# Diagonal masks of attention: from VectorE's minimum on the exponentials to TensorE's addition on the scores

## The reference

```
att = einsum('bhtd,bhsd->bhts', q, k) * scale
causal = triu(ones((T, T), bool), k=1)
att = where(causal, -inf, att)
att_prob = softmax(att, axis=-1)
att_v = einsum('bhts,bhsd->bhtd', att_prob, v)
return att_v @ w_out.T + b_out
```

## Time and profile before

| | |
|---|---|
| median of 3 runs | 4427.25 us (4421.09 to 4436.3) |
| the profiled execution's own time | 4430.29 us |
| its span | 4428.6 us |
| mean granted TensorE clock | 0.907 of 2.4 GHz |
| PE busy | 3624.9 us (82%), 23244 matmuls |
| DVE busy | 2584.7 us (58%) |
| ACT busy | 1880.7 us (42%) |
| POOL busy | 834.9 us (19%) |

### The profile page before, as it was taken

One profiled execution on the slowest core, in us unless ns is written; L12 is line 12 of the kernel. 1 busy time (PEld: TensorE's weight loads), 2 busy tenths in 40 slices (PEclk: granted clock), 3 DMA queues, 4 the chain that ended last, 5 costly groups with the idle time before them and its releaser, 6 DMA issues. The chain is left out here.

```text
span 4428.6 us, 62889 instructions
## 1 busy us (share of the span) xinstructions
PE 3624.9 (82%) x23244; PEld 2176.7 (49%) x23244; DVE 2584.7 (58%) x5480; ACT 1880.7 (42%) x2902; POOL 834.9 (19%) x1018
## 2 busy tenths in 40 slices
PE   5876786778768889888893889887988988898897
PEld 3424333334256373553732666656653653663672
DVE  5746666647555464554556555455665664765764
ACT  2262361452656556464662434343126125216216
POOL 3012111120122030120300323232311220220220
PEclk8887897888889999899996989998999999999999
DMA  5312403214140000000002000002000000000000
GB/s 189 120 38 68 130 29 111 86 59 121 41 154 1 5 25 6 24 1 29 1 6 79 5 24 29 5 24 79 1 1 30 1 1 29 1 1 30 1 1 11
DMA packets 147088, 177.11 MB, mean 40 GB/s; under 512 B 16384, under 2 KB 123392, under 8 KB 146688
## 3 DMA queue, kind: packets, MB, share of 16 engines
q1 hardware_dynamic: 139008, 153.81, 11.0%
q0 software_dynamic: 6144, 16.79, 1.2%
q10 hardware_dynamic: 1632, 2.49, 0.2%
HBM read 126.40 MB, written 51.38 MB: 40 GB/s over the span
## 5 line engine op out<-in xcount | busy, mean ns | idle before, releaser
L741 DVE TENSOR_REDUCE arena<-ps 128x2 f32<-128x1024 f32 (+3 forms) x768 | 698.8, 952 | 167.7 <-PE ps L709 94.8
L937 ACT ACTIVATE arena<-ps 128x1024 f32<-128x1024 f32 (+3 forms) x768 | 577.4, 812 | 236.9 <-PE ps L846 187.1
L1020 DVE TENSOR_TENSOR arena<-arena,tri 128x256 f32<-128x256 f32 x512 | 209.0, 422 | 329.1 <-ACT arena L937 317.4
L846 PE MATMUL ps<-arena 64*128 64x512 f16 (+3 forms) x1536 | 260.0, 353 | 139.4 <-ACT arena L937 89.4
L937 ACT ACTIVATE attention<-ps 128x1024 f32<-128x1024 f32 (+3 forms) x384 | 287.9, 809 | 187.3 <-PE ps L846 187.3
L863 PE MATMUL ps<-arena 128*17 128x512 f32 (+3 forms) x3072 | 349.4, 529 | 14.3 <-DVE arena L1020 12.2
L2591 ACT ACTIVATE arena<-ps 128x256 f32<-128x256 f32 x192 | 63.6, 381 | 620.2 <-PE ps L2533 575.0
L846 PEld LDWEIGHTS ps<-arena 64*128 64x128 f16 x1536 | 71.3, 94 | 496.2 <-ACT arena L937 387.5
L863 PE MATMUL ps<-attention,live 128*33 128x512 f32 (+3 forms) x1536 | 290.6, 502 | 0.0
L709 PE MATMUL ps<-arena 64*128 64x512 f16 (+3 forms) x1536 | 237.3, 335 | 50.4 <-DVE arena L741 31.6
L1190 PE MATMUL ps<-gated_parts,weight_parts 128*128 128x256 f32 x1536 | 219.0, 300 | 30.0 <-DVE operands L1291 30.0
(11 more groups left out here) (330 smaller groups left out, 7054.0 us busy)
## 6 DMA issues: line engine op xcount, KB each, us to landing
arena<-w_experts SPq DMA_DIRECT2D x128, 256.0 KB
acc<-sums SPq DMA_DIRECT2D x16, 1024.0 KB, 5.7
x_next<-sums SPq DMA_DIRECT2D x16, 1024.0 KB, 8.3
arena<-slots_x SPq DMA_DIRECT2D x32, 512.0 KB, 4.6
slots_y<-arena SPq DMA_DIRECT2D x32, 512.0 KB, 4.3
sums<-acc SPq DMA_DIRECT2D x24, 512.0 KB, 2.9
making<-basis SPq DMA_DIRECT2D x16, 768.0 KB, 6.3
slots_x<-arena SPq DMA_DIRECT2D x1, 4096.0 KB, 29.4
```

The costliest lines, as they stand in the source:

```text
L741: dve.reduce_max(a.mp[:, 2 * j:2 * j + 2, qt, c], out[:, :, 0:w], AX.X).then_inc(self.pair_out, 1)
L846: last = pe.matmul(m.ps[:, 4 + 2 * (v % 2) + odd, q0:CH], a.k[half, pair, kt * P:(kt + 1) * P], a.q[half, pair, c * CH + q0:(c + 1) * CH], ...
L937: act.activation(a.p[:, v % ring, :, q0:CH], m.ps[:, b:b + 2, q0:CH], ACT.Exp, scale=HD ** -0.5).then_inc(exped, 1)
L1020: dve.tensor_tensor(diag, diag, keep, ALU.min).then_inc(masked, 1)
```

## The change

`m.tri` becomes `m.above`, a bf16 tile of 0 where the key may be seen and -1.0e30 elsewhere. Behind each diagonal score pair TensorE now issues two more matmuls, one for each map, whose stationary operand is the unit matrix `m.ident_b` (128 x 128, bf16) and whose moving operand is `m.above` (128 columns); they add the triangle to the first 128 columns of the scores just made. The exponential then gives zero there. VectorE's minimum, its semaphore `masked` and TensorE's wait for it are gone.

```
@@ setup_constants
-            pool.memset(m.tri[:, :], KEEP).then_inc(cleared, 1)
+            pool.memset(m.above[:, :], 0.0).then_inc(cleared, 1)
-            pool.affine_select(out=m.tri[:, :], in_=m.tri[:, :], compare_op=ALU.is_ge, fill=0.0,
+            pool.affine_select(out=m.above[:, :], in_=m.above[:, :], compare_op=ALU.is_ge, fill=NEG,
                                base=0, pattern=[[1, P]], channel_multiplier=-1).then_inc(selected, 1)
@@ attention, TensorE, score(v)
                     last = pe.matmul(m.ps[:, 4 + 2 * (v % 2) + odd, q0:CH], a.k[half, pair, kt * P:(kt + 1) * P],
-                                     a.q[half, pair, c * CH + q0:(c + 1) * CH], start=True, stop=True)
+                                     a.q[half, pair, c * CH + q0:(c + 1) * CH], start=True, stop=not on_diagonal(n),
+                                     skip_group_check=True)
+                if on_diagonal(n):
+                    for odd in range(2):
+                        last = pe.matmul(m.ps[:, 4 + 2 * (v % 2) + odd, q0:q0 + P], m.ident_b[:, :], m.above[:, :],
+                                         start=False, stop=True, skip_group_check=True)
                 last.then_inc(scored, 1)
@@ attention, TensorE, values(n)
                 pe.wait_ge(exped, pairs * (n + 1))
-                if on_diagonal(n):
-                    pe.wait_ge(masked, pairs * diagonals[n + 1])
@@ attention, VectorE
-                for v in range(2 * block, 2 * block + 2) if block < n_blocks else ():
-                    n = v // pairs
-                    q0 = first_query(n)
-                    if on_diagonal(n):
-                        dve.wait_ge(exped, v + 1)
-                        diag = a.p[:, v % ring, :, q0:q0 + P]
-                        dve.tensor_tensor(diag, diag, keep, ALU.min).then_inc(masked, 1)
```

More of the change, by code:

```diff
@@ L805, in first_query @@
         return max(kt * P, c * CH) - c * CH
-    diagonals = [sum(on_diagonal(i) for i in range(n)) for n in range(n_units + 1)]
-    with stage(nc, "scored", "exped", "masked", "summed", "evac", "turned", "steps", "given", "y_turned", "y_stored",
+    with stage(nc, "scored", "exped", "summed", "evac", "turned", "steps", "given", "y_turned", "y_stored",
                "projected", "added", *(NextNormalisation.SEMAPHORES if store is not None else ()),
                pool=routed is not None) as \
-            (block, scored, exped, masked, summed, evac, turned, steps, given, y_turned, y_stored, projected, added,
+            (block, scored, exped, summed, evac, turned, steps, given, y_turned, y_stored, projected, added,
              *next_sems):
@@ L942, in _ @@
             step = Steps(dve, steps)
-            keep = m.tri[:, :].unsqueeze(1).broadcast_to([P, 2, P])
             def add(t):
@@ L2703, in program @@
         m.mask_col = sb("mask_col", [P, 2, P], BF16)
-        m.tri = sb("tri", [P, P], BF16)
+        m.above = sb("above", [P, P], BF16)
         m.ones_col = sb("ones_col", [P, 1])
```

## The result

The changed kernel takes 4508.63 us (median of 4 runs, 4505.7 to 4510.07) against 4424.17 us of the kernel before beside it: a ratio of 1.0185 (95% interval 1.0169 to 1.02), 84 us slower. The forecast was slower by 38 us; the direction and the range hold, and the loss is more than twice the forecast.

The account below looks back on a forecast made before the run. TensorE was taken to bound layer 1 and share layers 0 and 3 with ScalarE. Added matmuls 76.0 us less 37.6 given back made +38.4, predicted 4466 us; range for 8 in 10: 4422 to 4525.

Parts of the forecast that it names:

- What bounds the kernel: Attention stages: TensorE bounds layer 1 and shares layers 0 and 3 with ScalarE; VectorE is least loaded.
- The price of a pair, 0.111 us: Two added matmuls behind a diagonal score pair cost 0.056 us each, as the L479 turns do, weight loads hidden.
- The rival: Behind score pairs, the unit matrix's loads are exposed: 0.216 us a pair, +110 us in all, 4538; chance 0.14.
- a pair above 0.16 us: Sign named beforehand, for the added matmul pairs, that the unit matrix's weight loads are exposed.
- The count of pairs on the path, 49, 60 and 52 of 64: Diagonal pairs per stage of layers 0, 1 and 3 that lengthen it: 5.4 (6.5 with half clock), 6.7 and 5.8 us.
- ten pairs' worth for the half clock: Layer 0, mostly first chunk: ten pairs run at half clock, adding 1.1 us a stage, 6.5 in place of 5.4.
- The give-back, 37.6 us: TensorE's waits for VectorE that go: 4.4, 1.5 and 3.5 us a stage in layers 0, 1 and 3, four stages each.
- The sum: Whole kernel: 76.0 us of added matmuls less 37.6 us given back, +38.4 us, predicted 4466.
- the first rival: TensorE's waits for ScalarE in the attention stages take the masks: 22 us faster, 4405; chance 0.20.
- The clock: Denser TensorE work shortens layer 0's half-clock stretches, some 6 us a stage: 4441; sign, clock above 0.88; chance 0.06.
- The last rival: Later exponentials replace the direct mask waits, 3 us over a stage of each: +50, 4477; inside the forecast's 0.60.
- The Trainium skill: For added matmuls of 128 columns: about 81 ns each, an estimated 0.16 us a pair, sum near +72 us; not followed.

Follow-up runs that it names:

- unmasked: Diagonal masks left out altogether, on neither VectorE nor TensorE, against the kernel before: 4369.04 us, ratio 0.9876; repeated on another chip, 4261.61 us, 0.9876.
- first group: First of three sets of runs, each on its own chip and compared within itself; its kernel before took 4424.40 us (median).
- the third's: Third set of runs, on its own chip: kernel before 4316.48 us, changed kernel 4395.48, without masks 4261.61, four half-row matmuls behind scores 4295.33, ahead 4295.46.
- doubled masks: Triangle added twice, four matmuls behind each diagonal score pair in place of the changed kernel's two: 4587.83 us, 79 us over the changed kernel.
- the corners: Four kernels against the one before: before 0, no masks -55 us, TensorE's masks added with VectorE's work kept +115 (4539.35 us), changed +84.

## Why the prediction was right or wrong

Layer 1 is the cleanest gauge, since TensorE is busy nearly throughout there. Its unmasked stages take 106.7 us on the first group's chip and 106.7 to 107.0 on the third's, so stages of all groups stand side by side, less 106.7 and over 64:

| behind each diagonal score pair | stage of layer 1, us | a pair, us |
|---|---|---|
| nothing | 106.7 | |
| two, half the rows, 128 columns | 109.7 | 0.047 |
| four, half the rows, 64 columns | 109.8 | 0.048 |
| two, all rows, 8 columns | 116.1 | 0.147 |
| two, all rows, 128 columns (the change) | 120.4 | 0.214 |
| four, all rows, 128 columns | 127.0 | 0.317 |

The last column is net: in the kernels with more work TensorE also waited less.

*What bounds the kernel.* Right: work was moved to the engine with least room, and layer 1, where TensorE bounds outright, pays most.

*The price of a pair, 0.111 us.* Wrong, and it is the term that failed: in the trace it is 0.22 us where values follow and 0.31 where other scores follow. The L479 rows told truly what such matmuls cost behind one another and before other instructions on all rows. But in attention they stand between scores on 64-row halves and values on column groups. Each change between these uses of the array costs about 0.105 us beyond the columns, on the way to all rows as well as back. These are the start-to-start times in the kept traces (the lower quartile of each kind, so that waits do not count):

| from | to | us | its columns at 2.4 GHz | beyond them |
|---|---|---|---|---|
| scores of 256, half rows | other scores | 0.12 | 0.107 | 0.01 |
| scores of 256, half rows | masks on half rows | 0.12 | 0.107 | 0.01 |
| scores of 256, half rows | values, column groups | 0.21 | 0.107 | 0.106 |
| scores of 256, half rows | masks on all rows | 0.215 | 0.107 | 0.108 |
| two masks on all rows | scores | 0.218 | 0.107 | 0.111 |
| two masks on all rows | values | 0.216 | 0.107 | 0.109 |
| two masks on all rows | turns L383, all rows | 0.122 | 0.107 | 0.015 |

Where values follow, there was one change already (scores to values) and there are two now: 0.111 + 0.105. Where scores follow there was none and there are two now: 0.111 + 2 x 0.1. In the changed kernel 328 mask groups stand before scores, 368 before values and 72 before turns or projections on all rows. This shows the turns L383 start 0.12 us after the masks, and the values 0.21:

```profile
4425.57 0.28 PE L850 MATMUL ps<-above,ident_b 128*128 128x128 bf16 x2
4425.69 0.61 PE L383 MATMUL ps<-ident,xn 128*128 128x128 f32 x4
4426.23 0.23 PE L845 MATMUL ps<-arena 64*128 64x128 f16 x2
4426.40 0.28 PE L850 MATMUL ps<-above,ident_b 128*128 128x128 bf16 x2
4426.61 0.84 PE L865 MATMUL ps<-arena 128*17 128x384 f32 x8
```

I had seen 0.105 us between scores and values, took it for two exposed loads that every score pair pays, and then argued that the unit matrix would not have them. The rows of before spoke against the first half already: at 4334.70 a pair of 256 and one of 128 reach the values after 0.27 us, 0.16 for their columns and 0.11 once, not twice. The rival had the right number, 0.216, for the pairs that values follow, but for another reason: it let each load be exposed, and the doubled masks refute that. So a pair above 0.16 us, which I had named as the sign of exposed loads, could not tell the two causes apart.

*The count of pairs on the path, 49, 60 and 52 of 64.* Somewhat too high. Changed less unmasked is 10.9 us a stage in layer 0, 13.8 in layer 1 and 10.4 in layer 3, 140 us in all. By the prices above (0.31 before scores, 0.22 before values, 0.12 before work on all rows) all 768 pairs would cost an estimated 190 us, 0.25 each, so about a quarter was absorbed. At each layer's own mean price (0.25, 0.27 and 0.23 us) the stages grew by 44, 51 and 44 pairs of 64. Layer 1, where I had left 4 pairs to be absorbed, took up some 3 of an estimated 17 us. TensorE's waits for ScalarE there went from 3.6 us to 1.6:

```profile
PE ps L845 <- ACT attention L939: 1.6, 5, 0.4
```

In layer 0 I had added ten pairs' worth for the half clock. Its stages grew by no more than half a microsecond beyond those of layer 3, and the clock rose there from 0.84 to 0.89 in the stages compared.

*The give-back, 37.6 us.* Low when nothing else changes (55), and near when TensorE has its new work (31 by the corners). Two errors met: the waits gone were larger than I read from the rows, and by the corners 24 us of them are not given back when TensorE has the masks.

*The sum.* 76 - 38 = +38 predicted; 140 - 55 = +84 measured. A stage of layer 1 grew by 12 us where I had about 5, and the quartet takes 6.91 us where I had 6.2. With the mean price of 0.25 us on my own count (161 pairs a set of three stages, 644 in all) the working would have given 161 - 38 = +123, about 4550 and outside the range. That the range held is in part luck: the price was too low by more than half, and a count too high and a give-back too low made up for some of it.

*The other rivals.* The waits for ScalarE took part of the masks, as the first rival had it, but not most: in the last stage of layer 3 they went from 6.7 to 4.5 us, 2.2 of an estimated 15 us that 64 pairs cost. Where the rest of what was absorbed lies is not settled. The clock did rise in layer 0, as that rival had it, and at 0.87 to 0.90 it reached about the mark of 0.88 I had set, but doubled masks raised it likewise (0.90) while taking longer; whatever the clock gave back was less than the added work took. How many us that was is not settled. The last rival, that the waits for masks come back as waits for a later exponential, is not borne out: values wait for nothing in the list of layer 3.

*The Trainium skill.* "TensorE: Matmul & The Clock Gate", section "Back-to-back issue gap", gives about 81 ns a matmul, which had made an estimated +72 us. The total came nearer to that than to mine, yet the mechanism is not a rate: the second couple adds 0.055 us a matmul in the trace (0.33 us for four, 0.22 for two), and each change of the array's use 0.105 us once. Section "The mechanism" has loads overlap only where row groups differ. The doubled masks contradict that for operands on all rows: two more matmuls, each with its load, add 0.11 us, where their columns alone are 0.107.

## What to carry to other kernels

A price read from a row holds with its neighbours: look not only at the same shape but at what stands before and after it, start to start, above all whether the matmuls use the same rows and column groups of the array. Count these changes before and after the edit, each way. If a few small matmuls must be put between others that use half the rows, cut them to the same halves, even if that takes twice as many. And moving work off an engine that others seldom wait for buys only those waits; here 311 us of VectorE's time were worth 31 to 55.

## What the runs showed of the hardware that was not expected

- Each change between matmuls on 64-row halves, on all 128 rows and on column groups cost 0.10 to 0.11 us beyond the columns, in every direction measured (scores to masks, masks to scores, scores to values, masks to values); a follower that used the array in the same way started 0.01 to 0.02 us after the columns. Half-row operands of the same 128 columns cost a net 0.047 us a pair in layer 1, not 0.214.
- The changes can be read in the kernel before too: 0.12 us from scores of 256 columns to other scores, 0.21 to values.
- Shorter matmuls did not raise the clock: with 8 columns two of the four stages of layer 3 ran at 0.91, where the unmasked and the 128-column kernels had 0.96 to 0.98. This is one execution.
- The chip of the first group took 2.5% longer for the kernel before than the other two, and about half of that lies in the attention stages of layer 0: unmasked stages of 93.7 us at a clock of 0.86 on one, of 79.7 at 0.95 on the other. On the first, ScalarE waits 9 to 12 us a stage for a remote cause, in stages where GpSimd gathers; on the other the waits listed have no such row. What causes it was not tried. The effect of the change was nearly the same on either kind, 84 and 79 us.

Not tried: gathering the masks of several pairs, or placing them where the use of the array changes anyway, so that fewer changes are paid. Nor VectorE's masks in layer 1 with half-row masks in layers 0 and 3; by the stages, 108.3 us against 109.8, that would save some 6 us more, an estimate from one execution of each.
